# Two FP4 feed-forwards: last rounding step and residual addition moved to GpSimd, identity product dropped, down product one tile later in two halves

## What is computed

```python
def fp4_quant_dequant(x):              # BLOCK = 16, along the last dimension
    xb = x.reshape(shape[:-1] + (shape[-1] // BLOCK, BLOCK))
    scale = jnp.max(jnp.abs(xb), axis=-1, keepdims=True) / 6.0
    scale = jnp.maximum(scale, jnp.float32(1e-12))
    xn = xb / scale
    idx = jnp.searchsorted(_MID, jnp.abs(xn))
    q = _GRID[idx] * jnp.sign(xn) * scale
...
def fp4_linear(x, w):
    return jnp.einsum('bsk,nk->bsn', fp4_quant_dequant(x), fp4_quant_dequant(w))
...
gate = fp4_linear(x, w_gate)           # 256 -> 704
y = fp4_linear(x, w_up)
h = jax.nn.silu(gate) * y
return fp4_linear(h, w_down)           # 704 -> 256
...
x = x + _L1_ffn_ref(_layernorm(x, axis=-1), ...)
x = x + _L1_attn_b_ref(_layernorm(x, axis=-1), ...)
x = x + _L1_ffn_ref(_layernorm(x, axis=-1), ...)
```

## Time and profile before

| | us |
|---|---|
| median of 3 runs | 4081.86 (4077.23 to 4085.93) |
| the profiled execution | 4082.73 |
| its span in the profile | 4080.9 |
| first feed-forward, first to last product (L2555) | 2847.5 to 3160.4 |
| second feed-forward, first to last product | 3757.8 to 4064.1 |
| TensorE busy | 3623.4 (89%) |
| VectorE busy | 2915.8 (71%) |
| ScalarE busy | 1929.7 (47%) |
| GpSimd busy | 1633.9 (40%) |

### The profile page before, as it was taken

How to read it: one execution, slowest core, us unless ns; L and a number is a source line. 1 busy time by engine, 2 the same in 40 slices (tenths; PEclk the granted TensorE clock), 3 DMA queues, 4 the chain that set the end, 5 groups by cost and what they waited for, 6 DMA issues and landing times. The chain is left out here.

```text
span 4080.9 us, 60197 instructions
## 1 busy us (share of the span) xinstructions
PE 3623.4 (89%) x19256; PEld 2605.9 (64%) x19256; DVE 2915.8 (71%) x5355; ACT 1929.7 (47%) x4079; POOL 1633.9 (40%) x1485
## 2 busy tenths in 40 slices
PE   4888878999599999998799788987999899999998
PEld 3455557889488888887789634544666455554666
DVE  5777657676566666645677578886888676766998
ACT  3565644444455555544344344442444466656332
POOL 3776726454566666633555411101003445441000
PEclk8999979999899999998899889989999899999999
DMA  5999902565100000001266400002102444441000
GB/s 136 303 256 275 304 32 73 167 202 170 48 19 17 19 19 19 19 2 38 95 186 195 154 24 17 19 11 43 21 0 49 91 111 101 103 110 25 11 15 16
DMA packets 228874, 358.33 MB, mean 88 GB/s; under 512 B 36482, under 2 KB 132851, under 8 KB 221811
## 3 DMA queue, kind: packets, MB, share of 16 engines
q1 hardware_dynamic: 204038, 265.38, 22.4%
q0 software_dynamic: 24544, 89.36, 9.0%
HBM read 173.82 MB, written 172.20 MB: 85 GB/s over the span
## 5 line engine op out<-in xcount | busy, mean ns | idle before, releaser
L2895 DVE TENSOR_REDUCE ab_nmx<-banks 128x1 f32<-128x512 f32 x512 | 329.3, 684 | 136.6 <-PE banks L2682 134.2
L2826 ACT ACTIVATE ab_pt<-banks 128x512 f32<-128x512 f32 x512 | 283.2, 600 | 162.0 <-PE banks L2692 152.9
L1737 POOL TENSOR_TENSOR lb_pq<-lb_pq,lb_rr 128x512 f32<-128x512 f32 x192 | 206.2, 1077 | 305.1 <-DVE lb_rr L1598 301.7
L1463 ACT ACTIVATE lb_pq<-banks,lb_nmx 128x256 f32<-128x256 f32 x384 | 178.5, 470 | 230.0 <-DVE lb_nmx L1593 226.8
L2692 PE MATMUL banks<-ab_qT,ab_kT 128*128 128x512 f32 x512 | 253.2, 500 | 5.3 <-ACT ab_pt L2826 5.3
L358 ACT ACTIVATE da_pt<-banks 128x512 f32<-128x512 f32 (+1 forms) x384 | 179.1, 537 | 123.4 <-PE banks L270 119.1
L1593 DVE TENSOR_REDUCE lb_nmx<-banks 128x2 f32<-128x512 f32 x192 | 131.1, 683 | 146.5 <-PE banks L1315 145.2
L2682 PE MATMUL banks<-ab_kT,ab_qT 128*128 128x512 f32 x512 | 209.1, 411 | 18.5 <-DVE ab_nmx L2895 13.7
L285 PE MATMUL banks<-da_pt,da_vx 128*64 128x512 f32 (+3 forms) x1024 | 166.3, 470 | 34.4 <-POOL da_pt L578 30.8
L576 POOL TENSOR_TENSOR da_pt<-da_pt,w_da_tri 128x384 f32<-128x384 f32 x128 | 150.4, 1175 | 87.0 <-ACT da_pt L358 86.9
L2466 PE MATMUL banks<-w_f_dT,f_hT 128*128 128x256 f32 x768 | 178.3, 382 | 4.0 <-ACT f_hT L2512 4.0
(11 more groups left out here) (538 smaller groups left out, 11180.4 us busy)
## 6 DMA issues: line engine op xcount, KB each, us to landing
moe_xs<-zero SPq DMA_DIRECT2D x71, 512.0 KB, 11.5
...
da_spill<-da_hi SPq DMA_DIRECT2D x128, 128.0 KB, 2.4
ab_spill<-ab_hi SPq DMA_DIRECT2D x128, 128.0 KB, 2.4
...
```

The lines of the kernel that those rows point to most:

```text
L1463: nc.scalar.activation(pq[:, n % RING, t, :], ps[:, S_BANK + n % 2, 2 * P * t:2 * P * t + 2 * P], ACT.Exp, bias=nmx[:, n % RING, t:t + 1], ...
L1737: nc.gpsimd.tensor_tensor(pq[:, n % RING, :, :], pq[:, n % RING, :, :], bcast(rr[:, n % RING, :], 2, 2 * P), ALU.mult).then_inc(s_p, 1)
L2826: nc.scalar.activation(pt[:, s % RING, :], ps[:, EXP_BANK + s % 3, :], ACT.Exp, scale=AB_D ** -0.5).then_inc(s_e, 1)
L2895: nc.vector.tensor_reduce(nmx[:, g % 2, col:col + 1], ps[:, MAX_BANK + n % 3, :], op=ALU.max, axis=AX.X, negate=True).then_inc(s_mx, 1)
```

## The change

- The ninth rounding step (values times the block's scale) leaves VectorE. GpSimd does it, in two instructions: first x of t+2 (256 columns), then h of t (704 columns), each with a semaphore of its own (`s_qx`, `s_qh`). VectorE's step 3 of the next tile waits for `s_qh`, since it overwrites `v`. The scale has two buffers.
- The identity product is gone. The down product starts its bank afresh, ScalarE copies it into a new tile `y`, and GpSimd adds `y` to the residual.
- The down product of tile t-1 stands in step t, three of its six chunks ahead of the transposes of x and three behind; the transposes of h stand between gate and up.
- ScalarE's step ends with silu; the copy of the product of t-1 stands ahead of the copies of h. In f1 the statistics are those of tile t-2, stand ahead of the copy of x, and have a pass more (the sum, which came with the copy before).
- All this holds for tiles 0 to 19 of f1 and all tiles of f2. In tiles 20 to 31 of f1, where GpSimd works for the attention, VectorE does step 8 (in two pieces) and TensorE the identity product, in the new order.
- GpSimd's program runs f1's tiles first, then the attention, then f2's tiles. The attention's pieces between f1's tiles begin behind tile 23 rather than 22 (the first four are one tile later), its square roots stand behind ScalarE's step 22 (was 20) and the reciprocal behind VectorE's step 22 (was 21).

```diff
@@ class FeedForward @@
+    def by_pool(self, t, d=0):
+        return not isinstance(t, int) or t + d < self.pooled
...
+    def turn_h(self, pe, t, k):
+        pe.wait_ge(self.s_qh, t + 1)
...
+    def down(self, pe, t, d, k, parts=(0, 1)):
+        nc, ps, w = self.nc, self.ps, self.w
+        whole = self.by_pool(t, d)
+        if 0 in parts:
+            if self.known(t, -d + 1):
+                pe.wait_ge(self.s_pad, 1)
+            elif self.by_pool(t, d - 1):
+                pe.wait_ge(self.s_yc, t + d)
+            else:
+                pe.wait_ge(self.s_res, t + d)
+            if not whole:
+                nc.tensor.matmul(ps[:, 3, 0:C], self.core.ident[:, :], self.res[:, t + d, :], start=True, stop=False)
+            pe.wait_ge(self.s_hT, t + d + 1)
+        for m in [m for m in range(F4_IC) if 2 * m // F4_IC in parts]:
+            last = nc.tensor.matmul(ps[:, 3, 0:C], self.hT[:, k, m, :], w["f4_dT"][:, m, :], start=(whole and m == 0),
+                                    stop=(m == F4_IC - 1))
...
+    def pe_step(self, pe, t, k):
+        if self.there(t, -1):
+            self.down(pe, t, -1, 1 - k, (0,))
         if self.there(t, 2):
-            self.gate_up(pe, t + 2, k)
...
+            self.turn_x(pe, t + 2, k)
+        if self.there(t, -1):
+            self.down(pe, t, -1, 1 - k, (1,))
+        if self.there(t, 2):
+            self.gate(pe, t + 2, k)
+        self.turn_h(pe, t, k)
+        if self.there(t, 2):
+            self.up(pe, t + 2, k)
...
+    def take_y(self, act, t, d, k):
+        nc = self.nc
+        act.wait_ge(self.s_y, t + d + 1)
+        if self.by_pool(t, d):
+            if not self.known(t, 2 - d):
+                act.wait_ge(self.s_res, t + d - 1)
+            nc.scalar.copy(self.y[:, k, :], self.ps[:, 3, 0:C]).then_inc(self.s_yc, 1)
...
+    def statistics(self, act, t, d):
         nc, total, center, squares = self.nc, self.sums[:, 0:1], self.sums[:, 1:2], self.sums[:, 2:3]
+        act.wait_ge(self.s_res, t + d + 1)
+        nc.scalar.activation(self.square[:, :], self.res[:, t + d, :], ACT.Copy, accum_out=total)
         act.drain()
...
     def act_step(self, act, t, k, statistics):
         nc, ps = self.nc, self.ps
         if self.there(t, 3):
             self.normalised(act, t + 3, 1 - k)
+        if statistics and self.there(t, -2):
+            self.statistics(act, t, -2)
         if self.there(t, 2):
             self.copy_x(act, t + 2, k)
+        if self.there(t, -1):
+            self.take_y(act, t, -1, 1 - k)
         act.wait_ge(self.s_hTp, t + 1)
...
     def dve_step(self, dve, t, k):
...
+        wide = self.there(t, 2)
+        hi = F4_W if wide else F4_I
+        for step in range(8):
+            dve.drain()
+            if step == 0 and wide:
+                dve.wait_ge(self.s_xn, t + 3)
+            if step == 3 and not self.known(t, 1):
+                dve.wait_ge(self.s_qh, t)
+            last = self.step_of(step, k, 0, hi)
+        if self.by_pool(t):
+            last.then_inc(self.s_v, 1)
         else:
...
+    def pool_step(self, pool, t, k):
+        nc = self.nc
+        pool.wait_ge(self.s_v, t + 1)
+        for lo, hi, done in ((F4_I, F4_W, self.s_qx), (0, F4_I, self.s_qh)):
+            if lo and not self.there(t, 2):
+                continue
+            blocks = slice(lo // F4_BLK, hi // F4_BLK)
+            nc.gpsimd.tensor_tensor(fp4_blocks(self.both[:, k:k + 1, lo:hi]), fp4_blocks(self.v[:, :, lo:hi]),
+                                    bcast(self.sc[:, k, blocks], 2, F4_BLK), ALU.mult).then_inc(done, 1)
+        if self.there(t, -1):
+            self.add_y(pool, t, -1, 1 - k)
@@ def last_stages @@
-    head = {22: (-90, -88), 23: (-88, -86), 24: (-86, -84), 25: (-84, -76), 27: (-76, -58), 28: (-58, -38)}
+    head = {23: (-90, -88), 24: (-88, -86), 25: (-86, -84), 26: (-84, -76), 27: (-76, -58), 28: (-58, -38)}
...
+        f1 = FeedForward(core, w, ctx, own, "f4a", first_tiles, False, F4_TILES - 12)
+        f2 = FeedForward(core, w, ctx, own, "f4b", last_tiles, True, F4_TILES)
...
-                    if t == 20:
+                    if t == 22:
                         act.wait_ge(f1.s_rows, AB_EARLY * NT)
...
-                    if t == 21:
+                    if t == 22:
                         att.dve_scales(dve, 0, AB_EARLY, 1)
...
+                f1.pool_tiles(pool, 2)
                 att.pool(pool)
+                f2.pool_tiles(pool, 10)
```

133 lines of the change are left out of this document (73 added, 60 removed).

## The result

The changed kernel takes 4058.72 us in the median of five runs (4048.29 to 4062.79). The kernel before, run beside it, took 4081.86 (4077.23 to 4086.30). The ratio is 0.9945, 95% interval 0.9928 to 0.9963: 0.55% or 23 us faster.

A forecast was written before the change was run, and what follows sets the result against it. Two rings, TensorE's and VectorE's, both hanging on ScalarE's result copy, were taken as the bound. Second feed-forward -17.5 and first +3 make -14.5: 4082.73 becomes 4068.2, the median 0.87 lower, 4067 us; range 4048 to 4081.

The forecast's parts named there:

- Two rings on one copy: Second feed-forward before: TensorE's and VectorE's rings, within 0.3 us, both hang on ScalarE's result copy; shortening one brings at most 0.3.
- The second feed-forward: Ring over two tiles, 8.88 us from rounding's end to product t+2: 8.8 a tile against 9.55; -17.5 us in all.
- The price of GpSimd: GpSimd's last rounding step: 2.11 ns an element taken, 0.71 us for x and 1.66 for h.
- The port: Second feed-forward: VectorE loses 0.45 us a tile (0 to 0.9) to GpSimd's addition, at L2295 or L2298.
- The ten tiles beside the attention's tail: Start of the second feed-forward: each tile gains TensorE's 0.54 us, 5.5 us in all.
- The first feed-forward's ring: One-tile ring through silu, normalising, statistics, copy of x and gate: 9.4 us a tile against 9.70, -5.7 us.
- I am wrong about the statistics if the first stage runs at 8.8: Sign against the first feed-forward's forecast of ScalarE's statistics on the ring, with products 9.3 to 9.5 us apart.
- The roots: First feed-forward: attention's square roots come one tile later, the reciprocal idles VectorE 8 to 10 us; +8 us.
- about 0.3 each: +2: First feed-forward, tiles 23 to 29: the attention's jobs lengthen ScalarE's ring by about 0.3 us each, +2 us.
- The third rival: From 3.4 ns an element, GpSimd's products and addition run unbroken, L2291 waits: 10 us a tile, both stages, 4110; chance 0.17.
- V: Second feed-forward: end of the VectorE step before L2305, 0.07 us ahead of L2305's start; forecast times count from it.
- The second rival: GpSimd's runs of 16 cost 2.8 ns an element, 2.9 us for both products: 9.1 a tile, 4077; chance 0.16.

The follow-up runs named there:

- e3: Changed kernel, but the second feed-forward keeps only the down product's move, with identity product and last rounding step off GpSimd; 4077.16 us, ratio 0.9993.
- e4: Changed kernel, but the second feed-forward keeps only GpSimd's part, the down product whole in its own step again; 4085.14 us, ratio 1.0022.
- e1: Changed kernel with ScalarE's square root for the attention behind its step 21 instead of 22; 4048.63 us, ratio 0.9926.
- e2: Changed kernel with ScalarE's statistics between the copies of h and silu instead of ahead of the copy of x; 4053.29 us, ratio 0.9940.
- e8: Changed kernel with root behind step 21, statistics behind the copies of h, and VectorE's first two rotations one product later each; 4043.09 us, ratio 0.9906.
- e9: Changed kernel with root earlier, statistics behind h's copies, all three rotations one product later, GpSimd's addition two tiles back in both feed-forwards; 4028.39 us, ratio 0.9868.
- e6: Changed kernel, but GpSimd does its 704-element product twice in the second feed-forward; 4073.43 us, ratio 0.9985.

## Why the prediction was right, and where not

**Two rings on one copy.** Right, and the main step. e3 and e4 bear it out from both sides: 0.06 us (an estimated 0.13 with step 8 in one piece) and -0.07 us a tile for the halves, 0.84 for the pair.

**The second feed-forward, 8.8 us a tile and -17.5 in all.** It came to 8.72 and -20.4 with the tail. From the end of rounding to the product after next the chain took 8.78 us (3969.04 to 3977.82), 8.88 forecast. The price of GpSimd was mis-sized in the harmless direction: 2.11 ns an element was taken, since it stood nearest in length, and the rows gave the broadcast price (1.39 us for 704 elements, 0.62 for 256: 1.7 ns). The addition, with two full operands, took its 0.72 us as forecast. The port took 0.40 us a tile where 0.45 was forecast, on the two instructions named. The ten tiles beside the attention's tail gave 8.3 us in place of 5.5, since they too gained more than TensorE's 0.54, and the first gap gave 1.5 back (17.24 to 18.70), which is in part scatter: in e1 and e2, with the same second stage, it is 17.2, and the next one 1.0 longer.

**The first feed-forward's ring, 9.4 us.** The mechanism was right: VectorE and TensorE both idle 0.4 us, for silu and for the copy of x, and e2 takes the statistics off the ring and gets 8.84. The size was wrong: 9.05, so that nineteen tiles gave 10.8 us, not 5.7. VectorE was to idle nearly 1 us before each product; it idles 0.40, since the ring is shorter and since the addition costs it 0.38 us at L2295 in every tile. The failing step is the sum of ScalarE's terms, "silu 0.76, normalising 0.6, statistics 1.98, copy of x 0.37, hand-over 0.1", less about 0.1 of overlap. These are durations. From start to start the same four steps take 0.66, 0.49, 1.81 and 0.40 us, 3.36 in place of 3.7, since each of three instructions of ScalarE here starts some 0.1 us before the profile's end of the one ahead, 0.3 in all where 0.1 was allowed. The rest is the statistics, 1.90 us where 1.98 was put down, and the hand-over to gate, 0.05 for 0.1. "I am wrong about the statistics if the first stage runs at 8.8" lay on the right side of 9.05, but only just.

**The roots, +8 net.** The wait was foreseen in place and length: the reciprocal idles 8.23 us (8 to 10 forecast), and ScalarE then waits 7.19 for the transposes. Net it cost less. From product 22 to 25, 34.59 us became 38.06, +3.5. Two things were off. What the kernel before lost there was more than the 4 us that I put down (34.59 less three tiles of 9.7 is 5.5). And the stretched L2305, 3.15 us before, did not come back. It was not GpSimd's normalising that had stretched it, but the addition of a bias behind it (L2935 at 3070.45, 3.20 us). In the changed kernel this addition (now L3028 at 3074.03) begins under the second piece of step 8 and then lies under the product from PSUM and the reduction, which leave the port alone, so that step 8 ran in its 1.23 us. The normalising itself cost VectorE 0.4 us in all (L2298 0.86, L2300 0.69, L2302 1.35). That the bias addition cost nothing was luck of the moment: in e1 it meets L2304 and costs 2.0 us.

**What was missed.** The wait for the copies at the rotation, in the tiles for which "about 0.3 each: +2" was put down: the gap behind product 27 grew by 4.2 us. The step that failed is that the tables were costed by ScalarE's work alone. The diff shows the first four entries of TensorE's and ScalarE's table moved and none of VectorE's, and behind a moved piece hang SP's transfers, for which another engine waits. Before, the same rotation had a tile more for it: ScalarE made its input 10.6 us ahead of it, 4.8 in the changed kernel. The gap of before, 12.51 us in a ring of 9.7, was no sign of this, since there VectorE idled for the normalised x (1.23 us) and was held at the port (L2291 1.09 us for 0.19, L2295 1.71 for 1.16), and did not wait for copies. That products 25 to 31 came out 2.5 us longer, next to the +2 of the forecast, is luck: 4.2 us at this gap, and -1.7 in the others together.

**Between the stages, +4.7 where nothing was forecast.** Part is scatter. In the kernels whose first feed-forward is the changed one the distance from product 31 to the next stage's product 0 is 595.6 to 607.0 us. Of it, the way to the attention's first exponential took 48.0 us before and 49.0 to 51.4 in these six, 50.5 on average. In eight of the ten experiments, too, the median falls by 1.5 to 8.5 us less than both stages together do (in e4 it rises by 4.0 more). In e3, for one, they are 7.9 us shorter and the kernel 2.3 (interval -6.5 to +1.2). So a few microseconds of what the first feed-forward gains are given back behind it. Which transfer or engine takes them was not settled: in the changed kernel TensorE waits 5.05 us for the load of the attention's keys where it waited 3.38, but e8, with 5.13, reaches its first exponential as early as e9, with 3.13. In e9 the sum of both stages, 52.8 us, arrives in full (56.4).

**The third rival.** Its sum does not give its own threshold. At 3.4 ns the two products would take 0.34 + 3.26 us and end at V+3.7; to end at V+3.3, behind y's copy, 3.0 ns are enough. e6, whose products end 3.62 us behind V, is therefore well inside its condition, and the tile took 9.33 us, not 10: the step that failed is that L2291 would wait for the addition too. (The second rival's 2.9 us for both products at 2.8 ns come to 3.0 by the same sum.)

So the forecast of -14.5 us against -24.1 measured was cautious by 10.7 us in the first stage and by 2.9 in the second, and 4.7 went the other way between them, for a reason that it did not have. That the time lies only 8 us from the forecast owes something to that.
